# A Mamba block and a mixture of experts on one core: a new table of steps for the work beside the scan

## The chip, the core and the metric

The kernel runs on one core of a Trainium2 chip, in one launch. The metric is the device time of the launch in microseconds, lower is better. Everything is float32.

## The reference, cut to what matters

```python
# x: (8, 1024, 256); _layernorm without g, b is plain, with eps 1e-5
x = x + attn_block(_layernorm(x))
x = x + ffn_block(_layernorm(x))

# attn_block(x): Di = 512, 16 states, rank 64, 4 taps
h = _layernorm(x, ln_g, ln_b)
x_in, z = split(h @ W_in)
x_c = silu(causal_depthwise_conv(x_in, conv_w, conv_b))
dt, Bm, Cm = split(x_c @ W_xproj, [64, 80])
delta = softplus(dt @ W_dt + b_dt)
s = exp(delta * A) * s + delta * Bm * x_c          # along the sequence
y = sum(s * Cm, over the 16 states) + x_c * D_param
return x + (y * silu(z)) @ W_out

# ffn_block(x): 8 experts, the best 2 of each row, softmax over the two
logits = x @ Wg + bg
y = x + sum of w_e * (relu(x @ W1[e] + b1[e]) @ W2[e] + b2[e])
return gamma * (y - mean) * rsqrt(var + 1e-5) + beta
```

## The kernel before, in words

**Chunks, groups, steps.** The 8192 rows are cut into 16 chunks of 512. Even chunks begin a sequence and odd ones go on with it, so the states' last column is kept (`carry`) in an even chunk and read in the odd one. A chunk has 4 groups of 128 channels, a group has 16 states, and one state of one group is a step: 64 steps a chunk, 1024 in all. Each engine's program is one loop over the steps (`for at in range(STEPS)`, GpSimd over half-steps of two), and every other piece of work is put between the steps by a constant. Engines run each their own program; they meet at semaphores only, so a step number is a place in an engine's order and not a time.

**A step.** ScalarE makes the decay, `exp(delta * a)` (`exp_a`, L1156). GpSimd makes the drive, two states at a time (`times_b`, L852); for the states 4, 5, 10 and 11 TensorE does so with diagonal matrices (`drive`, L1462, at the group's steps 4 and 10; a chunk has its drives at 4, 10, 20, 26, 36, 42, 52, 58). VectorE scans (`scan`, L664). It then multiplies five pairs of states of a group by C (`weigh`, L676), and GpSimd the other three pairs (L869, behind a copy of the carry, L863). TensorE turns each pair and adds it up in `ps_y` (`turn_d`, L1435, `turn_p`, L1445; `TURN_D` and `TURN_P` say at which step), after `begin_y` (L1426) has put the skip term there. VectorE gates the sum at the next group's step 3 (`gate`, L686). State 0 reuses the bank of state 15, so ScalarE can't start a group before VectorE has scanned the last state of the one before.

**Work beside the steps.** `STEADY` lists the projections and turns of a chunk as (kind, g, chunk relative to the current one, TensorE's first step, in how many parts, how many steps after it ScalarE takes the result out). Kinds: h (the normalised rows turned, L1318), x and z (L1324, L1328), conv (four taps as matmuls, L1335), dbc and bturn (dt, B, C; B turned for the diagonals), dt (L1346), turnu (delta*u turned for the drives, L1381), back (the gated rows turned back, L1390), out (L1400, L1404), turnx, logit (L1353, L1357, L1361) and rank (the router's). The list is sorted by first step plus parts, and its results take turns in the two banks of `ps_p`: a use waits until the one two places before it has been taken out (`project`, `emptied`). In the last step before 64 a copy may fall into the next chunk.

**The other constants.** `NORM`, `STATS`, `INV_STD`: the first layer norm of the chunk two ahead. `ADD_DT`: the last softplus step on VectorE. `SILU_U`, `SILU_Z`: SiLU with two loads of ScalarE's table each. `XL_AT`: the residual. `STATS_X1`, `INV_STD_X1`, `FACTOR_X1`, `XN`: squares, reciprocal deviation, the product for the offset (`factors_x1`, L818, GpSimd, counted in half-steps) and the normalisation (`normalise_x1`, L1001) of the last chunk's rows before the router. `ROUTE`: VectorE's fourteen small router instructions (`route_step`, L592 to L619), the steps of each; from one to the next it waits on its own semaphore. `EXP_W`, `IDS_0`, `IDS_1`, `SCATTER`: the two weights, the rows' numbers, and the stores of the rows by expert. `DIAGONALS`: the diagonal matrices of B (`diagonals`, L1109), four parts. `HALO_AT`: the three columns that the convolution needs of the chunk before. They are written out as numbers; nothing in the kernel reckons costs or due times. `RESIDUAL` is read nowhere.

The loops that place the work on ScalarE look like this:

```python
for kind, g, q, at, parts, lag in table:
    if at >= 0 and kind in (...):
        empty_at.setdefault(at + lag, []).append((kind, g, q))
# in the loop over the steps: empties first, then the norms, last
for k in keep_at.get(at, ()):
    keep(k)
exp_a(c, s // N, s % N)
```

Of the kernel before, what the change touches and what calls it, by code (L numbers as in the profile page):

```python
# [111 lines left out]
def mamba_block(nc, x_t, x1_t, b_dram, ln_g, ln_b, W_in, conv_w, conv_b, W_xproj, W_dt, b_dt, A_log, D_param,  # L112
# [25 lines left out]
    with ExitStack() as ctx:  # L138
        def sb(name, shape, dt=F32):
            return ctx.enter_context(nc.sbuf_tensor(name, shape, dt))  # L140

        def sem(name):
# [30 lines left out]
        dbc = sb("dbc", [K_DT, CH])  # L173
# [108 lines left out]
        OUT_EARLY = NC * SG - 5  # L282
        SPIN_FIRST = {"dbc": 8, "bturn": 3, "turnu": 12}
        SPIN_LAST = {"out": 4, "turnx": 14, "logit": 4, "rank": 4}
        STEADY = [("h", 0, 1, 0, 1, 3), ("h", 1, 1, 1, 1, 5), ("back", 3, -1, 6, 1, 3), ("x", 0, 1, 7, 2, 3),
                  ("dt", 2, 0, 8, 1, 2), ("out", 0, -1, 11, 2, 3), ("turnu", 1, 0, 12, 1, 4), ("x", 1, 1, 14, 1, 6),
                  ("out", 1, -1, 16, 2, 6), ("x", 2, 1, 21, 1, 3), ("conv", 0, 1, 22, 1, 2), ("x", 3, 1, 23, 2, 2),
                  ("conv", 1, 1, 23, 4, 6), ("dt", 3, 0, 27, 1, 3), ("conv", 2, 1, 27, 3, 5),
                  ("turnu", 2, 0, 34, 1, 2), ("conv", 3, 1, 32, 4, 7), ("turnx", 0, -1, 37, 1, 4),
                  ("turnx", 1, -1, 37, 1, 4), ("logit", 0, -1, 40, 1, 4), ("dbc", 0, 1, 41, 1, 3),  # L290
                  ("bturn", 0, 1, 42, 1, 4), ("back", 1, 0, 42, 1, 4), ("rank", 0, -1, 44, 1, 0),
# [3 lines left out]
        HALO_AT = 0  # L295
        XL_AT = 11
        SILU_U = 41
        SILU_Z = 73
        NORM = (54, 58)
        ADD_DT = ((49, 0), (51, 1), (74, 2), (95, 3))  # L300
        RESIDUAL = ((10, 0), (4, 1))
        STATS = (47, 48)
        INV_STD = (51, 54, 55)
        FACTOR = 28
        STATS_X1 = (26, 27)
        INV_STD_X1 = (28, 28)
        FACTOR_X1 = 17
        XN = (34, 38)
        ROUTE = (38, 39, 40, 40, 40, 41, 41, 41, 41, 41, 45, 45, 45, 45)
        EXP_W = (44, 46, 46)  # L310
        IDS_0 = 46
        IDS_1 = 58
        SCATTER = ((25, 0, 0), (25, 0, 1), (27, 0, 2), (28, 0, 3), (32, 1, 0), (33, 1, 1), (35, 1, 2), (38, 1, 3))
        DIAGONALS = (54, 57, 61, 63)
        DRIVE = (4, 4, 10, 10)
        KEEP_EARLY = (4, 9)
        GATE = 3
        TURN_D = {9: 0, 11: 1, 14: 2, 15: 3, 19: 4}
        TURN_P = {9: 0, 15: 1, 20: 2}
        SKIP_Y = 7  # L320
        WEIGH_P = {5: 0, 8: 1, 10: 2}
# [3 lines left out]
        def due(at, offset, d, span=SG):  # L325

            c, rest = divmod(at - offset, span)
            return c + d if rest == 0 and 0 <= c + d < NC else None

        uses = sorted([(*u, 0) for u in START] + [(*u, NC - 1) for u in END] + [(*u, None) for u in STEADY],  # L330
                      key=lambda u: u[3] + u[4])
# [228 lines left out]
        def _(dve):  # L560
# [179 lines left out]
            for at in range(STEPS):  # L740
# [19 lines left out]
                for j, offset in enumerate(STATS):  # L760
                    q = due(at, offset, 2)
                    if q is not None:
                        (stats_a, stats_b)[j](q)
                for j, offset in enumerate(ROUTE):
                    q = due(at, offset, -1)
# [33 lines left out]
        def _(pool):  # L799
# [9 lines left out]
            def factors(q):  # L809

                pool.wait_ge(rs_done, 3 * q + 2)
                pool.tensor_tensor(nb[:, q % 3], rr[:, q % 3], nm[:, 0, :].unsqueeze(1).broadcast_to([P, 2, NT]),
                                   ALU.mult).then_inc(prm, 1)

            def factors_x1(q):

                pool.wait_ge(rsr_done, 2 * q + 2)
                pool.tensor_tensor(x_ln[:, 1, :], x_ln[:, 0, :], nm[:, 1, :], ALU.mult).then_inc(prm1, 1)  # L818
# [56 lines left out]
            for at in range(STEPS // 2):  # L875
# [20 lines left out]
                if q is not None and q > 1:  # L896
                    factors(q)
                q = due(at, FACTOR_X1, -1, G * HB)
                if q is not None:
                    factors_x1(q)  # L900
                for offset, k, i in SCATTER:
                    q = due(at, offset, -1, G * HB)
# [4 lines left out]
        def _(act):  # L907
            def set_halo(q):

                if q > 0:  # L910
                    act.wait_ge(proj_full, full("conv", 3, q - 1))
                if q == 1:
                    act.wait_ge(conv_step, TAPS * (G - 1))
                if q % 2 == 0:
                    act.memzero(xin[:, :, 0:HALO]).then_inc(halo, 1)
                else:
                    act.copy(xin[:, :, 0:HALO], xin[:, :, CH:CH + HALO]).then_inc(halo, 1)
# [314 lines left out]
            for at in range(STEPS):  # L1232
                c, s = divmod(at, SG)
                if s == HALO_AT and c + 1 < NC:
                    set_halo(c + 1)
# [19 lines left out]
                if q is not None:  # L1255
                    silu_gate(q)
                    act.preload_act_table_set("natural_log_exp_and_others")
                for j, offset in enumerate(INV_STD):
                    q = due(at, offset, 2)
                    if q is not None:  # L1260
                        inv_std(q, j)
                for j, offset in enumerate(STATS_X1):
                    q = due(at, offset, -1)
                    if q is not None:
                        stats_x1(q, j)
                for j, offset in enumerate(INV_STD_X1):
                    q = due(at, offset, -1)
                    if q is not None:
                        inv_std_x1(q, j)
                if s in NORM and c + 2 < NC:  # L1270
                    normalise(c + 2, range(2) if s == NORM[0] else range(2, NT))
                if s in XN and 0 < c <= NC and at != NC * SG + XN[1]:
                    normalise_x1(c - 1, range(2) if s == XN[0] else range(2, NT))
                for j, offset in enumerate(EXP_W):
                    q = due(at, offset, -1)
                    if q is not None:
                        weight_exp(q, j)
                for j, offset in enumerate(START_DIAGONALS):
                    if at == offset:
                        diagonals(0, 2 + j)  # L1280
                for j, offset in enumerate(DIAGONALS):
                    q = due(at, offset, 1)
                    if q:
                        diagonals(q, j)
                for k, offset in enumerate((IDS_0, IDS_1 if at < NC * SG else IDS_0)):
                    q = due(at, offset, -1)
# [13 lines left out]
        def _(pe):  # L1300
# [165 lines left out]
            def turns(t, n):  # L1466

                if 0 < t <= LAST + 1:
                    if n + N in TURN_D:
                        turn_d(t - 1, TURN_D[n + N])  # L1470
                    if n + N in TURN_P:
                        turn_p(t - 1, TURN_P[n + N])
                if t <= LAST:
# [3 lines left out]
                    if n == SKIP_Y:  # L1477
                        begin_y(t)
                    if n in TURN_D:
                        turn_d(t, TURN_D[n])  # L1480
                    if n in TURN_P:
# [445 lines left out]
```

## Time and profile before

| what | us |
|---|---|
| three runs | 2424.89, 2426.41, 2429.95 |
| median | 2426.41 |
| profiled execution | 2419.56 |
| its span | 2417.9 |
| VectorE, busy in the span | 2039.6 |
| TensorE (matmuls), busy | 2179.0 |
| GpSimd, busy | 1829.7 |
| ScalarE, busy | 1511.6 |

The span goes from the first to the last instruction of the profiled execution, and its time has some 2 us more around it. The busy shares are an average over two parts that are unlike: the scan up to 1802 us and, behind it, the experts, which TensorE fills. In the rows below PE is TensorE, PEld its weight loads, DVE VectorE, ACT ScalarE, POOL GpSimd. A bracket behind a row of a timeline is the time for which the engine was idle before it, and who ended that. The chunks are numbered from 0; chunk 6 starts at 706.10 us, chunk 7 at 815.33 us and chunk 8 at 926.12 us (VectorE's scan of step 0).

### The profile page before, as it was taken

How to read it: one execution, taken by the hardware profiler on the slowest of the kernel's cores; microseconds unless marked ns; L12 is line 12 of the kernel's file. 1: busy time of each engine (PE TensorE's matmuls, PEld its weight loads, DVE VectorE, ACT ScalarE, POOL GpSimd, SP SyncE). 2: the span in 40 equal slices, each digit the busy share in tenths (PEclk: the TensorE clock that was granted, in tenths of full speed). 3: DMA queues.
4: the chain of work that ended last, by engine and by line, in shares of the span. 5: the costliest groups of instructions: out<-in, count | busy, mean ns of one | idle time of the engine just before them, and what ended most of it. 6: DMA issues, size and time to landing. Idle time of an engine off the chain costs nothing. (4 is left out here: it accounts for less than half of the span.)

```text
span 2417.9 us, 47511 instructions
## 1 busy us (share of the span) xinstructions
PE 2179.0 (90%) x13721; PEld 1761.9 (73%) x13722; DVE 2039.6 (84%) x3049; ACT 1511.6 (63%) x3296; POOL 1829.7 (76%) x1093
## 2 busy tenths in 40 slices
PE   8889899998989899998989898999787999999980
PEld 5667677776767777766777776667676999999970
DVE  5999999999999999999999999999984555555558
ACT  6687877878787877878787878778741111111106
POOL 3888989889898989898898989898972444444447
PEclk9999999999999999999999999999988999999995
DMA  5041423314041413223140413132238999999978
GB/s 173 9 134 50 136 69 108 114 63 159 27 158 38 139 61 125 93 83 137 47 158 22 156 50 136 64 112 100 69 111 222 229 233 226 232 227 228 230 165 278
DMA packets 186792, 312.51 MB, mean 129 GB/s; under 512 B 18851, under 2 KB 118083, under 8 KB 186500
## 3 DMA queue, kind: packets, MB, share of 16 engines
q1 hardware_dynamic: 140932, 258.53, 33.8%
q0 software_dynamic: 25584, 34.62, 7.5%
q10 hardware_dynamic: 20112, 17.32, 2.2%
q8 instruction: 85, 1.39, 0.2%
q14 instruction: 79, 0.65, 0.1%
HBM read 247.09 MB, written 63.32 MB: 128 GB/s over the span
## 5 line engine op out<-in xcount | busy, mean ns | idle before, releaser
L852 POOL TENSOR_TENSOR dbu<-drive_u,b_rows 128x1024 f32<-128x1024 f32 x384 | 905.1, 2365 | 82.9 <-DVE ss L664 32.2
L1156 ACT ACTIVATE ps_a<-delta,a_neg 128x512 f32<-128x512 f32 x768 | 518.1, 687 | 136.9 <-DVE ss L664 120.4
L869 POOL TENSOR_TENSOR wp<-ss,rows_c 128x1024 f32<-128x1024 f32 x192 | 454.0, 2364 | 35.8 <-DVE ss L664 35.2
L1764 POOL DMA_INDIRECT acc_scratch<-ow,idx x135 | 212.1, 1571 | 306.5 <-issue 140.0
L676 DVE TENSOR_TENSOR wd<-ps_a,rows_c 128x1024 f32<-128x1024 f32 x320 | 385.6, 1205 | 0.0
L1435 PEld LDWEIGHTS ps_y<-ident,wd 128*128 128x128 f32 x2560 | 299.8, 143 | 100.0 <-issue 71.0
L1435 PE MATMUL ps_y<-ident,wd 128*128 128x128 f32 x2560 | 337.2, 277 | 13.5 <-DVE wd L676 13.2
L1802 ACT COPY e_meta<-xt 128x2 f32<-128x2 f32 x135 | 26.1, 193 | 437.4 <-PE e_ps_x L1875 250.5
L1462 PEld LDWEIGHTS ps_a<-dg,duT 128*128 128x128 f32 x2048 | 251.8, 198 | 56.8 <-issue 55.5
L1462 PE MATMUL ps_a<-dg,duT 128*128 128x128 f32 x2048 | 261.4, 283 | 29.8 <-ACT carry L1163 27.3
L1686 DVE TENSOR_SCALAR e_hT<-e_ps_h,b_turned 128x128 f32<-128x128 f32 x540 | 152.1, 345 | 142.0 <-PE e_ps_h L1884 124.5
L1884 PE MATMUL e_ps_h<-xT,b_rows 128*128 128x128 f32 x2160 | 263.3, 275 | 0.3 <-ACT xT L1804 0.3
L1893 PE MATMUL e_ps_o<-rows_c,e_hT 128*128 x1080 | 255.3, 379 | 0.0
L664 DVE TENSOR_TENSOR_SCAN ss<-ps_a,carry,dbu 128x512 f32<-128x512 f32 x192 | 243.9, 1270 | 11.5 <-ACT ps_a L1156 11.5
L1884 PEld LDWEIGHTS e_ps_h<-xT,b_rows 128*128 128x128 f32 x2160 | 251.9, 192 | 0.6 <-ACT xT L1804 0.6
L664 DVE TENSOR_TENSOR_SCAN ss<-ps_a,dbu 128x512 f32<-128x512 f32 x192 | 232.1, 1209 | 22.6 <-ACT ps_a L1156 20.6
L664 DVE TENSOR_TENSOR_SCAN ps_a<-ps_a,carry,dbu 128x512 f32<-128x512 f32 x192 | 238.8, 1282 | 0.7 <-issue 0.6
L664 DVE TENSOR_TENSOR_SCAN ps_a<-ps_a,dbu 128x512 f32<-128x512 f32 x192 | 227.6, 1220 | 9.1 <-ACT ps_a L1156 7.2
L1335 PE MATMUL ps_p<-xin,taps 128*128 128x512 f32 x488 | 231.9, 593 | 0.8 <-ACT xin L1053 0.8
L1445 PE MATMUL ps_y<-ident,wp 128*128 128x128 f32 x1536 | 206.4, 279 | 15.7 <-POOL wp L869 15.0
L1893 PEld LDWEIGHTS e_ps_o<-rows_c,e_hT 128*128 128x128 f32 x1080 | 194.9, 190 | 21.0
L1445 PEld LDWEIGHTS ps_y<-ident,wp 128*128 128x128 f32 x1536 | 178.1, 143 | 30.9 <-POOL wp L869 22.9
(200 smaller groups left out, 3650.9 us busy)
## 6 DMA issues: line engine op xcount, KB each, us to landing
b_rows<-in_L_ffn_W_dram SPq DMA_DIRECT2D x135, 512.0 KB
rows_c<-b_scratch SPq DMA_DIRECT2D x128, 512.0 KB, 5.1
b_rows<-b_scratch SPq DMA_DIRECT2D x96, 512.0 KB, 4.1
xt<-xs_scratch SPq DMA_DIRECT2D x135, 129.0 KB
xb<-in_L_attn_x_dram SPq DMA_DIRECT2D x16, 512.0 KB, 4.0
hx<-in_L_attn_x_dram SPq DMA_DIRECT2D x16, 512.0 KB, 6.4
x_scratch<-hx SPq DMA_DIRECT2D x16, 512.0 KB, 2.9
acc_scratch<-stage SPq DMA_DIRECT2D x16, 512.0 KB, 2.9
```

What stands on the lines that cost most here:

```text
L664: dve.tensor_tensor_scan(dst, decay, drive, init, ALU.mult, ALU.add).then_inc(scan_done, 1)
L676: dve.tensor_tensor(wd[:, s % NWD], states(k, 2), cc[:, n:n + 2, :], ALU.mult).then_inc(wd_done, 1)
L852: pool.tensor_tensor(dbu[:, k % NBU], du[:, g % 2, :].unsqueeze(1).broadcast_to([P, 2, CH]), bb[:, row:row + 2, :], ALU.mult).then_inc(dbu ...
L869: pool.tensor_tensor(wp[:, s % 2], ss[:, s % 2], cc[:, rows, :], ALU.mult).then_inc(wp_done, 1)
L1156: act.activation(dst, dl[:, g, :], ACT.Exp, scale=a_neg[:, g, n:n + 1]).then_inc(exp_done, 1)
L1335: ins = pe.matmul(dst, taps[:, g, k, :], xin[:, g, k:k + CH], start=(k == 0), stop=(k == TAPS - 1))
L1435: ins = pe.matmul(ps_y[:, i, :], wd[:, s % NWD, h, i * P:(i + 1) * P], ident[:], start=False, stop=False, is_transpose=True, skip_group_ch ...
L1445: ins = pe.matmul(ps_y[:, i, :], wp[:, s % 2, h, i * P:(i + 1) * P], ident[:], start=False, stop=(j == 2 and h == 1 and i == NT - 1), is_t ...
L1462: ins = pe.matmul(ps_a[:, bank(k), i * P:(i + 1) * P], duT[:, i, :], dg[:, p, h, i, :], start=True, stop=True)
L1764: pool.indirect_dma_start(out=acc_dram, out_offset=bass.IndirectOffsetOnAxis(ap=idx[:, old, :], axis=0), in_=ow[:, old, :], in_offset=None ...
L1884: ins = pe.matmul(ps_h[:, 1 - par, j, :], w1[:, (slot + 3) % RING, k, j * P:(j + 1) * P], xT[:, 1 - par, k, :], start=(k == 0), stop=(k == ...
L1893: ins = pe.matmul(ps_o[:, par, 0:D], hT[:, par, k, :], w2[:, bass.ds((e * KF + k) * D, D)], start=(k == 0), stop=(k == KF - 1))
```

## The change

It alters constants in the table of steps and nothing else: which step of a chunk each piece of work has in its engine's order, in how many parts TensorE does it, and how many steps later ScalarE takes it out. No instruction's operands change, and none is added or taken away, but for where a projection is cut into parts.

```diff
--- before.py
+++ after.py
@@ -282,40 +282,40 @@
         OUT_EARLY = NC * SG - 5
         SPIN_FIRST = {"dbc": 8, "bturn": 3, "turnu": 12}
         SPIN_LAST = {"out": 4, "turnx": 14, "logit": 4, "rank": 4}
-        STEADY = [("h", 0, 1, 0, 1, 3), ("h", 1, 1, 1, 1, 5), ("back", 3, -1, 6, 1, 3), ("x", 0, 1, 7, 2, 3),
-                  ("dt", 2, 0, 8, 1, 2), ("out", 0, -1, 11, 2, 3), ("turnu", 1, 0, 12, 1, 4), ("x", 1, 1, 14, 1, 6),
-                  ("out", 1, -1, 16, 2, 6), ("x", 2, 1, 21, 1, 3), ("conv", 0, 1, 22, 1, 2), ("x", 3, 1, 23, 2, 2),
-                  ("conv", 1, 1, 23, 4, 6), ("dt", 3, 0, 27, 1, 3), ("conv", 2, 1, 27, 3, 5),
-                  ("turnu", 2, 0, 34, 1, 2), ("conv", 3, 1, 32, 4, 7), ("turnx", 0, -1, 37, 1, 4),
-                  ("turnx", 1, -1, 37, 1, 4), ("logit", 0, -1, 40, 1, 4), ("dbc", 0, 1, 41, 1, 3),
-                  ("bturn", 0, 1, 42, 1, 4), ("back", 1, 0, 42, 1, 4), ("rank", 0, -1, 44, 1, 0),
-                  ("back", 0, 0, 45, 1, 2), ("turnu", 3, 0, 46, 1, 2), ("dt", 0, 1, 48, 1, 0), ("dt", 1, 1, 49, 1, 3),
-                  ("z", 0, 1, 54, 1, 1), ("z", 1, 1, 57, 1, 2), ("z", 2, 1, 58, 2, 6), ("turnu", 0, 1, 60, 1, 2),
-                  ("back", 2, 0, 62, 1, 4), ("z", 3, 1, 61, 2, 5)]
-        HALO_AT = 0
+        STEADY = [("h", 0, 1, 0, 1, 3), ("h", 1, 1, 0, 1, 5), ("back", 3, -1, 6, 1, 3), ("x", 0, 1, 7, 2, 3),
+                  ("dt", 2, 0, 8, 1, 2), ("out", 0, -1, 11, 1, 2), ("turnu", 1, 0, 12, 1, 4), ("x", 1, 1, 14, 1, 6),
+                  ("out", 1, -1, 15, 2, 6), ("x", 2, 1, 20, 1, 3), ("conv", 0, 1, 22, 1, 3), ("x", 3, 1, 23, 2, 2),
+                  ("conv", 1, 1, 23, 4, 6), ("dt", 3, 0, 26, 1, 3), ("conv", 2, 1, 27, 3, 5),
+                  ("turnu", 2, 0, 34, 1, 3), ("conv", 3, 1, 31, 4, 7), ("turnx", 0, -1, 37, 1, 4),
+                  ("turnx", 1, -1, 37, 1, 4), ("logit", 0, -1, 39, 1, 5), ("dbc", 0, 1, 41, 1, 4),
+                  ("back", 1, 0, 42, 1, 4), ("rank", 0, -1, 42, 1, 0), ("back", 0, 0, 46, 1, 2),
+                  ("turnu", 3, 0, 46, 1, 2), ("bturn", 0, 1, 47, 1, 3), ("dt", 0, 1, 49, 1, 0),
+                  ("dt", 1, 1, 49, 1, 3), ("z", 0, 1, 54, 1, 1), ("z", 1, 1, 54, 2, 3), ("turnu", 0, 1, 58, 1, 2),
+                  ("z", 2, 1, 58, 2, 6), ("back", 2, 0, 60, 1, 3), ("z", 3, 1, 60, 2, 5)]
+        HALO_AT = 5
         XL_AT = 11
         SILU_U = 41
         SILU_Z = 73
-        NORM = (54, 58)
+        NORM = (55, 58)
         ADD_DT = ((49, 0), (51, 1), (74, 2), (95, 3))
-        RESIDUAL = ((10, 0), (4, 1))
+        RESIDUAL = ((10, 0), (0, 1))
         STATS = (47, 48)
-        INV_STD = (51, 54, 55)
+        INV_STD = (53, 54, 54)
         FACTOR = 28
-        STATS_X1 = (26, 27)
-        INV_STD_X1 = (28, 28)
-        FACTOR_X1 = 17
-        XN = (34, 38)
-        ROUTE = (38, 39, 40, 40, 40, 41, 41, 41, 41, 41, 45, 45, 45, 45)
-        EXP_W = (44, 46, 46)
-        IDS_0 = 46
-        IDS_1 = 58
-        SCATTER = ((25, 0, 0), (25, 0, 1), (27, 0, 2), (28, 0, 3), (32, 1, 0), (33, 1, 1), (35, 1, 2), (38, 1, 3))
-        DIAGONALS = (54, 57, 61, 63)
+        STATS_X1 = (25, 26)
+        INV_STD_X1 = (26, 27)
+        FACTOR_X1 = 18
+        XN = (35, 37)
+        ROUTE = (38, 40, 40, 40, 40, 41, 41, 41, 41, 41, 45, 45, 45, 45)
+        EXP_W = (44, 46, 47)
+        IDS_0 = 47
+        IDS_1 = 59
+        SCATTER = ((25, 0, 0), (25, 0, 1), (26, 0, 2), (27, 0, 3), (32, 1, 0), (33, 1, 1), (35, 1, 2), (38, 1, 3))
+        DIAGONALS = (54, 57, 61, 64)
         DRIVE = (4, 4, 10, 10)
         KEEP_EARLY = (4, 9)
         GATE = 3
-        TURN_D = {9: 0, 11: 1, 14: 2, 15: 3, 19: 4}
+        TURN_D = {9: 0, 11: 1, 12: 2, 18: 3, 20: 4}
         TURN_P = {9: 0, 15: 1, 20: 2}
         SKIP_Y = 7
         WEIGH_P = {5: 0, 8: 1, 10: 2}
```

## Rows read from the trace of the kernel before

**Rows 1.** one stretch: length, busy us of PE, PEld, DVE, ACT, POOL, PEclk, DMA

```profile
40.00:1802.00 1762.00, 1617.15 (x9871) 1246.39 (x9872) 1670.84 (x1791) 1373.31 (x2830) 1555.40 (x881) 0.98 0.28 95
```

**Rows 2.** waits of VectorE, 40 to 1802: us in total, times, longest

```profile
DVE ss L664 <- ACT ps_a L1156: 32.1, 21, 2.1
DVE delta L636 <- ACT delta L1127: 26.1, 16, 3.0
DVE ps_a L664 <- PE ps_a L1462: 13.5, 17, 1.4
...
DVE mx L592 <- PE ps_p L1361: 3.4, 8, 0.8
DVE ps_a L664 <- POOL dbu L852: 1.8, 1, 1.8
```

**Rows 3.** timeline, VectorE, chunk 6: start, us, what [idle before]

```profile
745.38 1.23 DVE L664 TENSOR_TENSOR_SCAN ps_a<-ps_a,dbu 128x512 f32<-128x512 f32 x1 [0.59 <-ACT ps_a L1156]
748.75 1.22 DVE L664 TENSOR_TENSOR_SCAN ss<-ps_a,dbu 128x512 f32<-128x512 f32 x1 [2.14 <-ACT ps_a L1156]
...
751.83 2.34 DVE L664 TENSOR_TENSOR_SCAN ps_a<-dbu,ps_a 128x512 f32<-128x512 f32 x2 [0.74 <-PE ps_a L1462]
...
772.84 0.19 DVE L592 TENSOR_REDUCE mx<-ps_p 128x4 f32<-128x32 f32 x1 [0.38 <-PE ps_p L1361]
...
774.08 0.17 DVE L594 TENSOR_TENSOR ps_p<-ps_p,mx 128x32 f32<-128x32 f32 x1
774.16 1.22 DVE L664 TENSOR_TENSOR_SCAN ps_a<-ps_a,dbu 128x512 f32<-128x512 f32 x1
```

**Rows 4.** timeline, TensorE, chunk 6, drives of steps 10 and 26

```profile
718.97 2.02 PE L1462 MATMUL ps_a<-dg,duT 128*128 128x128 f32 x16 [0.58 <-ACT carry L1163]
...
750.74 1.95 PE L1462 MATMUL ps_a<-dg,duT 128*128 128x128 f32 x16
```

**Rows 5.** timeline, GpSimd, chunk 6 and chunk 7

```profile
757.22 0.19 POOL L818 TENSOR_TENSOR x_ln<-x_ln,nm 128x4 f32<-128x4 f32 x1
...
759.96 2.37 POOL L869 TENSOR_TENSOR wp<-ss,rows_c 128x1024 f32<-128x1024 f32 x1
...
869.48 2.37 POOL L869 TENSOR_TENSOR wp<-ss,rows_c 128x1024 f32<-128x1024 f32 x1 [2.93 <-DVE ss L664]
```

**Rows 6.** timeline, ScalarE, chunk 6 and chunk 7

```profile
761.36 1.08 ACT L1001 ACTIVATE stage<-hx,x_ln 128x256 f32<-128x256 f32 x2
762.35 1.29 ACT L1156 ACTIVATE ps_a<-delta,a_neg 128x512 f32<-128x512 f32 x2
...
769.23 1.07 ACT L1076 COPY xb<-ps_p 128x512 f32<-128x512 f32 x2 [0.17 <-PE ps_p L1353]
...
870.74 1.09 ACT L1001 ACTIVATE stage<-hx,x_ln 128x256 f32<-128x256 f32 x2
...
878.51 1.07 ACT L1076 COPY xb<-ps_p 128x512 f32<-128x512 f32 x2 [0.15 <-PE ps_p L1353]
```

**Rows 7.** timeline, TensorE, chunk 6, first matmul of the logits

```profile
770.45 0.40 PE L1357 MATMUL ps_p<-bgb,ones 1*128 1x32 f32 x2
```

**Rows 8.** timeline, VectorE, behind the scan

```profile
1819.55 0.20 DVE L594 TENSOR_TENSOR ps_p<-ps_p,mx 128x32 f32<-128x32 f32 x1
1819.78 0.22 DVE L596 TENSOR_TENSOR_SCAN cn<-first,ps_p 128x32 f32<-128x32 f32 x1
```

**Rows 9.** timeline, TensorE, starts of chunks 6 and 8

```profile
707.06 1.14 PE L1318 MATMUL ps_p<-ident,hx 128*128 128x128 f32 x8 [1.90 <-ACT zt L1098]
...
927.08 1.45 PE L1318 MATMUL ps_p<-ident,hx 128*128 128x128 f32 x8 [1.91 <-ACT zt L1098]
```

**Rows 10.** timeline, VectorE, chunk 8, steps 4 and 9

```profile
931.72 0.69 DVE L686 TENSOR_TENSOR zt<-ps_y,zt 128x512 f32<-128x512 f32 x1
932.56 2.34 DVE L664 TENSOR_TENSOR_SCAN ps_a<-dbu,ps_a 128x512 f32<-128x512 f32 x2
...
939.80 1.22 DVE L664 TENSOR_TENSOR_SCAN ss<-ps_a,dbu 128x512 f32<-128x512 f32 x1 [0.43 <-ACT ps_a L1156]
```

## The prediction

> **What bounds the kernel now.** I read the stretches first: the scan runs from 40 to 1802 us, VectorE is busy for 1670.8 of those 1762 us and TensorE for 1617.2 [rows 1]. None of the changed constants acts on the experts behind it, which fill the rest of the span, so they are costed at nothing. The scan is 16 chunks of 64 steps, some 110 us each, and what can move is the 91 us in which VectorE is idle (1762 less 1670.8) and whatever the new order adds. The waits of VectorE say who ends them [rows 2]: ScalarE's exponentials (32.1 us), the softplus of dt 2 (26.1), TensorE's drive products (13.5), the router's logits (3.4). GpSimd ended one wait of a drive, 1.8 us: it is ahead, and its moved scatters cost nothing as long as that lead stands.
>
> The timeline of VectorE shows the places in one chunk (chunk 6, even; all even chunks look alike, and the odd ones nearly so) [rows 3]: at step 25 it waits 2.14 us for ScalarE, at step 26 another 0.74 us for TensorE, at step 38 0.38 us for the logits. TensorE's timeline tells what stands behind the first two [rows 4]. It waits once, 0.58 us for a carry copy behind SiLU, starts the drive at 718.97, and from there works without a break to the drive of step 26 at 750.74, on which the scan at 751.83 starts. The wait at step 25 lies inside this chain. Were it gone, VectorE would reach step 26 earlier and wait there instead. So up to step 26 a chunk is as long as TensorE's work, and only work taken out of that chain, or a wait put into it, counts.
>
> **The change part by part.** (1) *Steps 0 to 26.* x 2, out 0 and out 1 come a step earlier, turn 3 moves behind out 1 (15 to 18), turn 4 from 19 to 20, turn 2 from 14 to 12. Between the drive of step 10 and that of step 26 TensorE issues the same instructions as before in another order; no work leaves the chain. conv 0 is evacuated one ScalarE step later, so the exponential of step 24 no longer waits for it: its wait was inside the chain, worth nothing. STATS_X1 a step earlier puts four squares and a logarithm ahead of the exponential of step 26. That exponential now comes about level with the drive instead of well ahead of it. I take nothing, between nothing and the 0.74 us that VectorE waits there now, and nearer to nothing because the four squares and the logarithm together are hardly longer than the lead.
>
> (2) *The router's row factor.* FACTOR_X1 goes from GpSimd's half-step 17 to 18. At 17 it stood behind a product and ran at 757.22. At 18 it is issued behind the weighing of the third staged pair, which waits for the scan of step 31 and runs at 759.96 for 2.37 us, in the odd chunk at 869.48 [rows 5]. So it is done at 762.53 (759.96 + 2.37 + 0.20), in the odd chunk at 872.05. XN (34 to 35) waits for it. ScalarE began that normalisation at 761.36 and 870.74 [rows 6]: it is now 1.17 and 1.31 us late. Against this, one exponential (a pair takes 1.29 us, so 0.6 from start to start) now runs ahead of it, and the waits of 0.17 and 0.15 us before the copies of the turned rows are used up [rows 6]. That leaves 0.40 and 0.56 us. The logits' first matmul began at 770.45, 0.15 us after the copies' end at 770.30 (769.23 + 1.07), of which I count 0.1 as slack [rows 6, 7]: 0.30 and 0.46 us. I take 0.30 for both, since in the odd chunk ScalarE has more small waits to use up. VectorE waits for the logits already (0.38 us in rows 3), and in odd chunks they land with nothing to spare, so this is wholly exposed: 14 chunks x 0.30 = 4.2 us. Queued behind VectorE's maximum are the scans of 39 to 41. Bounds: 0 if ScalarE finds the time elsewhere, 14 x 0.46 = 6.4 us.
>
> (3) *ROUTE 39 to 40.* The compare with the maximum stood between two scans, independent of both: 774.08 to 774.16, 0.08 us [rows 3]. Now the router's next instruction, which reads its result and waits for its semaphore, stands directly behind it. That pair occurs at the end of the scan, 1819.55 to 1819.78: 0.23 us [rows 8]. So 0.15 us more on VectorE in each of 15 chunks: 2.25 us. Bounds: 0 and 15 x 0.23 = 3.5 us.
> The Trainium skill, page "VectorE: DVE Perf Modes", section "The DRAIN you can't avoid", says otherwise: a chain of vector operations with a semaphore after each took as long as one without, since the next has to wait for the pipe anyway. By it this part is 0 and the sum below 2.5 us; rows 3 and 8 speak against it, with two spacings for the same instruction.
>
> (4) *The end of a chunk and the start of the next.* z 1 goes from 57 to 54 in two parts, turn u 0 from 60 to 58, back 2 from 62 to 60 and its copy from ScalarE's step 2 to 63, h 1 from 1 to 0, the last diagonals from 63 to 64, halo to 5. At the start of an even chunk TensorE waited 1.90 us for the copy of back 2 (at 707.06). In chunks 4, 8 and 12 its granted clock then fell to the lower level: in chunk 8 the same eight turns took 1.45 us instead of 1.14 [rows 9], the drive came late, and VectorE lost 0.15 us at step 4 (the gate ends at 932.41, the scan starts at 932.56) and 0.43 at step 9 [rows 10]. With that copy made before the chunk ends h 0 doesn't wait; h 1 does, for z 3's copy, but 0.5 us less. I take the 0.58 us as gained in these three chunks: -1.7 us. Bounds: 0 and 7 x 0.58 = -4.1 us. The softplus wait of step 10 stays: SiLU and the residual hold it, and both start from the exponentials behind the weighing of step 3, which neither moves.
>
> (5) *Slots.* Projections alternate between two banks, so a new order gives new predecessors. dt 1 now waits for the copy of bturn (ScalarE's step 50), z 1 for the softplus sum of dt 1 on VectorE (step 51), z 3 for the copy of z 2 (step 0 of the next chunk), behind which stand turn 3, the turns of h and the drive of step 4. By the order of these steps TensorE waits a step or two in each place, where it waited as long elsewhere; none is on the path as long as the clock stays up. NORM, INV_STD, bturn, back 0, EXP_W and IDS move by one step or more on a ScalarE that is then a little ahead. rank two steps earlier, logit one: TensorE's order around them is unchanged where it binds. dbc's copy a step later delays SyncE's store of B and C and the loads queued behind it by a microsecond or two; the rows are wanted a third of a chunk later. All this I cost at 0. If the cover goes, it is rival A.
>
> Sum: 4.2 + 2.25 - 1.7 = +4.7 us. The profiled execution took 2419.56 us (its span 2417.9), 6.9 us below the median of the three runs, 2426.41. The terms are stalls that repeat in each chunk, so I add them to the median: **2431.1 us**. A measurement of this kernel can tell about 0.2%, 4.9 us, from no change; the forecast lies just inside that.
>
> **The rivals.** *A, slower.* The longer waits in (5) lower TensorE's clock just before the drive of step 4 in most chunks, not in three. The price is that of chunk 8, 0.58 us [rows 10], and a further 0.3 (1.45 less 1.14, rows 9) because the eight matmuls of turn 3 now stand in front of that drive as well: 0.9 x 14 = 12.6 us without the gain in (4), so 2426.4 + 6.4 + 12.6 = 2445 us if in all chunks, 2439 if in half. It decides from the point where the drive of step 4 is over 0.6 us later than now. For it: row 927.08. Against it: in four of seven even chunks the clock stayed up after a wait as long.
> The Trainium skill, page "TensorE: Matmul & The Clock Gate", section "HAM oscillation", says that gaps in matmul work bring the clock down to half each time; here it fell after one of the two waits in rows 9.
> *B, faster.* ScalarE, not TensorE, sets steps 24 to 26: the modelled ends of matmuls are late, the drive of step 26 is in fact ready, and conv 0 out of the way gives back what it cost. Even chunks wait 0.59 us at step 24 [rows 3]: 7 x 0.6 = 4.2 us, and the 0.74 us at step 26 shrink by half, 14 x 0.37 = 5.2. With the sum, 2431.1 - 9.4 = 2421.7 us. For it: the 32.1 us put down to ScalarE [rows 2]. Against it: TensorE's unbroken row [rows 4].
> *C, the order doesn't matter.* The positions have slack everywhere except in places that don't change, and the late logits are caught up by the waits of steps 41 and 42: 2426 us. The waits' regularity speaks against it.
> *D*, part (3) costs nothing: 2428.9 us.
>
> **How the numbers follow.** Forecast 0.33 (about half of it on either side of +0.2%), A 0.22, B 0.20, C 0.17, D 0.08. Faster is B and the low edge: 0.21. Within 0.2%: C, D and half of the forecast: 0.41. Slower: A and the other half, 0.38. The range reaches down to B, 2420, and up to A in half of the chunks, 2439.
>
> **What would show it.** In the changed kernel's trace: the drives of step 26 end in the same distance from step 3 (TensorE's row unbroken), VectorE's waits for logits rise from 3.4 to some 8 us in odd chunks too, GpSimd's small product of the row factor stands behind the weighing, the compare is 0.23 us ahead of the next router instruction, and the turns of h wait less than 1.9 us. Step 24 waits for nothing. It is wrong if chunks get shorter before step 26, or if the wait of step 4 grows in every chunk (A).

## The result, and the profile after

The changed kernel takes 2434.01 us (median of 7 runs, 2431.55 to 2436.24), the kernel before, run beside it, 2422.9 us (7 runs with the three shown above, 2420.47 to 2429.95). The ratio is 1.0037, 95% interval [1.0027, 1.0048]: slower by 9 us of 2423. (The medians of the two sets of seven are 11 us apart; where the two differ I go by the ratio and its interval.) The forecast was +4.7 us.

The profiled execution took 2431.55 us, its span 2429.8 against 2417.9. The first row has the busy times of the whole span. The second is the stretch of the scan, which now ends at 1812 instead of 1802 (columns as in [rows 1]).

```profile
PE 2190.3 (90%) x13721; PEld 1767.1 (73%) x13722; DVE 2040.4 (84%) x3049; ACT 1506.2 (62%) x3296; POOL 1827.0 (75%) x1093
```

```profile
40.00:1812.00 1772.00, 1626.91 (x9875) 1249.99 (x9876) 1671.89 (x1792) 1368.54 (x2831) 1553.70 (x880) 0.97 0.28 94
```

VectorE is busy for 1671.9 us where it was busy for 1670.8: of the 10 us more, 9 are waits. TensorE is busy for 10 us more with the same matmuls, and the mean granted clock is 0.97 instead of 0.98: those matmuls were slower. VectorE's waits up to 1812 us say where it shows (to be read against [rows 2]):

```profile
DVE ss L664 <- ACT ps_a L1156: 38.6, 19, 3.3
DVE delta L636 <- ACT delta L1127: 28.1, 18, 3.4
DVE ps_a L664 <- PE ps_a L1462: 18.4, 21, 1.5
...
DVE mx L592 <- PE ps_p L1361: 3.9, 8, 0.5
```

The first row has grown by 6.5 us, for the most part because the wait of step 25 took over those of step 24, as forecast in part (1). The third is new time: four waits more, 4.9 us more, the longest 1.5 us. To place it, I took the distance from the start of each of the 1024 scans of a step to the next in both traces and subtracted. All together are 10.2 us longer; by place in the chunk, summed over the 16 chunks:

| from the scan of step to the next | us | in which chunks |
|---|---|---|
| 41 to 42 (waits for the drive) | +7.4 | +1.36 in 3, +1.54 in 8, 10, 12, 14; 1 had it already |
| 39 to 41 (the compare) | +2.0 | 0.14 in each of 15 |
| 38 to 39 (the logits) | +1.6 | +0.09 to +0.18 in 1 to 14, -0.27 in 15 |
| 35 to 36 | +1.3 | +0.16 in even ones |
| 23 to 26 | +1.0 | +1.8 in 0, else -0.2 to +0.02 |
| 56 to 57 | +1.1 | 0, 2, 4 |
| 10 to 11 | -2.1 | -1.8 in 0 |
| 3 to 4 and 8 to 9 | -1.9 | -0.57 in 4, 8, 12 |

The rest adds up to -0.2 us, and behind the scan come 1.7 us more that no run looked into. The -1.8 us of chunk 0 stands in e1 below too, whose one change comes later than that, so it isn't the new order's. One place, which the prediction doesn't name, holds most of the difference between these two executions. This is TensorE's timeline there, in chunk 8 of the changed kernel, and VectorE's scan of step 42:

```profile
993.01 1.06 PE L1426 MATMUL ps_y<-skipd,xc 128*128 128x128 f32 x8
994.12 0.37 PE L1357 MATMUL ps_p<-bgb,ones 1*128 1x32 f32 x2
994.42 1.95 PE L1361 MATMUL ps_p<-wg,xb 128*128 128x8 f32 x16
996.23 1.07 PE L1435 MATMUL ps_y<-ident,wd 128*128 128x128 f32 x8
997.14 1.80 PE L1445 MATMUL ps_y<-ident,wp 128*128 128x128 f32 x8
998.74 4.56 PE L1341 MATMUL ps_p<-xc,wxp 128*96 128x512 f32 x8
1003.13 1.95 PE L1462 MATMUL ps_a<-dg,duT 128*128 128x128 f32 x16
```

```profile
1004.22 2.34 DVE L664 TENSOR_TENSOR_SCAN ps_a<-dbu,ps_a 128x512 f32<-128x512 f32 x2 [1.46 <-PE ps_a L1462]
```

In chunk 6, where nothing is lost, the turns of wp and the projection dbc take their usual times:

```profile
776.86 1.04 PE L1445 MATMUL ps_y<-ident,wp 128*128 128x128 f32 x8
777.74 3.60 PE L1341 MATMUL ps_p<-xc,wxp 128*96 128x512 f32 x8
```

So 0.76 us (1.80 less 1.04) and 0.96 us (4.56 less 3.60) are lost in a row, ahead of the drive that VectorE needs next. Two stretches of chunk 8, before the slow matmuls and over them (the last columns are the granted clock, the DMA share and GB/s):

```profile
993.80:997.20 3.40, 3.35 (x30) 3.15 (x29) 2.93 (x4) 3.37 (x3) 2.71 (x2) 1.00 0.00 0
997.25:1000.66 3.41, 3.41 (x12) 2.27 (x11) 3.31 (x7) 3.26 (x5) 2.35 (x1) 0.50 0.00 0
```

TensorE's clock is at its upper level of 2.4 GHz, then at the lower one, 1.2 GHz. TensorE did not wait before that, being busy for 3.35 of 3.40 us; but what it did were the logits, sixteen records with 8 moving columns each. The Trainium skill, page "TensorE: Matmul & The Clock Gate", section "HAM oscillation", ties the fall to idle gaps between matmuls; this row has next to no gap, so the trace doesn't agree. The kernel before has the same event once, in chunk 1 (dbc 4.77 us, a wait of 1.4 us, the "longest" of the third line of [rows 2]); the changed kernel has it in six chunks.

### The profile page after: what moved, and what is told of

Read it like the earlier page. It is cut to its first block and busy times, and to the rows that moved or that the text cites. A ratio compares the mean times of both kernels' runs of the same rounds, so it can differ in the third digit from the quotient of the medians.

```text
span 2429.8 us, 47511 instructions
## 1 busy us (share of the span) xinstructions
PE 2190.3 (90%) x13721; PEld 1767.1 (73%) x13722; DVE 2040.4 (84%) x3049; ACT 1506.2 (62%) x3296; POOL 1827.0 (75%) x1093
## 5 line engine op out<-in xcount | busy, mean ns | idle before, releaser
L1435 PE MATMUL ps_y<-ident,wd 128*128 128x128 f32 x2560 | 331.9, 278 | 8.6 <-DVE wd L676 8.0
L1462 PEld LDWEIGHTS ps_a<-dg,duT 128*128 128x128 f32 x2048 | 244.6, 194 | 35.8 <-issue 34.2
L1462 PE MATMUL ps_a<-dg,duT 128*128 128x128 f32 x2048 | 255.1, 278 | 15.1 <-ACT carry L1163 10.9
L1445 PE MATMUL ps_y<-ident,wp 128*128 128x128 f32 x1536 | 209.8, 282 | 13.2 <-POOL wp L869 13.2
L1445 PEld LDWEIGHTS ps_y<-ident,wp 128*128 128x128 f32 x1536 | 183.2, 146 | 43.6 <-issue 23.7
```

The costliest lines, as they stand in the source:

```text
L1435: ins = pe.matmul(ps_y[:, i, :], wd[:, s % NWD, h, i * P:(i + 1) * P], ident[:], start=False, stop=False, is_transpose=True, skip_group_ch ...
L1445: ins = pe.matmul(ps_y[:, i, :], wp[:, s % 2, h, i * P:(i + 1) * P], ident[:], start=False, stop=(j == 2 and h == 1 and i == NT - 1), is_t ...
L1462: ins = pe.matmul(ps_a[:, bank(k), i * P:(i + 1) * P], duT[:, i, :], dg[:, p, h, i, :], start=True, stop=True)
```

## The experiments

Each kernel was profiled in one execution, and chunks are counted in that one; how the count varies between executions of a kernel was not seen. Two theories. **Order**: TensorE's new order around steps 39 to 42 makes the clock fall. **Alignment**: the thin logits can bring the clock down in any of these kernels, and whether they do in a given chunk depends on when they come, so that any small shift changes the number of chunks hit. The first four kernels share 22 runs of the kernel before (median 2423.61 us, 2419.53 to 2427.11).

**e1, the compare alone.** Kernel before with

```diff
-        ROUTE = (38, 39, 40, 40, 40, 41, 41, 41, 41, 41, 45, 45, 45, 45)
+        ROUTE = (38, 40, 40, 40, 40, 41, 41, 41, 41, 41, 45, 45, 45, 45)
```

> The kernel before with the router's second instruction moved from step 39 to 40, nothing else. In the changed kernel VectorE needs about 0.14 us more at steps 40 and 41 of each chunk, and in six chunks TensorE's clock is low over step 41 and costs 1.4 to 1.5 us at step 42. Theory Alignment (the thin matmuls of the logits can lower the clock in any of these kernels; whether they do depends on when the stretch comes, which every small shift alters): 15 x 0.15 = +2.2 us from the instruction, and the places where the clock is low move; with low clock at step 41 in several chunks up to +7 us more. Theory Order (the new order of TensorE's work makes the stretch prone to it): +2.2 us and low clock at step 41 in chunk 1 only, as before.

2425.47 us, ratio 1.0007 [0.9997, 1.0017]. The scans of steps 39 and 40 are 0.08 us closer, those of 40 and 41 0.22 us further apart, in each of 15 chunks: +2.0 us. Part (3) stands. Two chunks (2 and 10) have the wait of 1.5 us at step 42, where the kernel before had one.

**e2, the row factor alone.** Kernel before with

```diff
-        FACTOR_X1 = 17
-        XN = (34, 38)
+        FACTOR_X1 = 18
+        XN = (35, 37)
```

> The kernel before with FACTOR_X1 at 18 and XN at 35 and 37, nothing else. My part (2): the logits come 0.3 us later in 14 chunks, +4.2 us. The changed kernel's trace shows only some 0.2 us at steps 36 to 39, so by its rows +2 to +3 us. Theory Alignment: low clock at step 41 in some chunks is possible here too, each +1.5 us; theory Order: none but chunk 1.

2432.85 us, ratio 1.0042 [1.0029, 1.0055]: as large as the whole loss, with TensorE's order untouched. (The profiled execution, 2437.66 us, was the slowest of its seven, that of the kernel before one of its fastest, so the two profiles lie further apart than the ratio.) Its chunk 6, GpSimd's factor, ScalarE's normalisation and VectorE's maximum:

```profile
763.31 2.38 POOL L869 TENSOR_TENSOR wp<-ss,rows_c 128x1024 f32<-128x1024 f32 x1
765.65 0.20 POOL L818 TENSOR_TENSOR x_ln<-x_ln,nm 128x4 f32<-128x4 f32 x1
...
765.89 1.09 ACT L1001 ACTIVATE stage<-hx,x_ln 128x256 f32<-128x256 f32 x2 [0.49 <-POOL x_ln L818]
...
776.47 0.19 DVE L592 TENSOR_REDUCE mx<-ps_p 128x4 f32<-128x32 f32 x1 [0.65 <-PE ps_p L1361]
```

The factor stands behind the weighing, as forecast, and the logits are waited for 0.65 us instead of 0.38 [rows 3]: 0.27 us more in even chunks, 0.19 in odd ones, 3.2 us in all. The other 11.7 us are at step 42, in chunks 2, 4, 6, 8, 10, 12 and 14 (1.67 us each; chunk 1 has it as before):

```profile
996.25 0.37 PE L1357 MATMUL ps_p<-bgb,ones 1*128 1x32 f32 x2 [0.24 <-ACT xb L1076]
996.55 1.95 PE L1361 MATMUL ps_p<-wg,xb 128*128 128x8 f32 x16
998.36 1.26 PE L1435 MATMUL ps_y<-ident,wd 128*128 128x128 f32 x8
999.41 1.92 PE L1445 MATMUL ps_y<-ident,wp 128*128 128x128 f32 x8
1001.12 4.29 PE L1341 MATMUL ps_p<-xc,wxp 128*96 128x512 f32 x8
```

```profile
999.10:1002.51 3.41, 3.41 (x14) 2.59 (x12) 3.34 (x7) 3.38 (x6) 2.35 (x1) 0.50 0.00 0
```

The theory Order falls: in this execution the old order is hit in eight chunks, behind a shift of 0.2 to 0.3 us.

**e3, all but those two.** Changed kernel with ROUTE, FACTOR_X1 and XN as before.

> The changed kernel with ROUTE, FACTOR_X1 and XN as before; the whole order of TensorE's work stays new. Theory Order: low clock at step 41 stays in five or six chunks, so only the two small parts come back, -2 to -4 us against the changed kernel, still 6 us or more above the kernel before. Theory Alignment: a chunk is 0.15 to 0.45 us shorter, the stretch comes at other times, and the number of chunks with low clock there is free to change, to none or to more; without any the time is within 2 us of the kernel before.

2427.68 us, ratio 1.0017 [1.0007, 1.0026], with the wait in five chunks (1, 8, 10, 12, 14), which both theories allow. Nothing is paid between steps 39 and 41; the logits come as before in even chunks and 0.16 us later in odd ones, which some other move does.

**e4, the end of a chunk alone.** Kernel before with h 1, z 1, turn u 0, back 2, z 3, HALO_AT, NORM, INV_STD, IDS_1 and the last of DIAGONALS as after.

> The kernel before with the changes at a chunk's end alone (h 1, z 1, z 3, turn u 0, back 2, halo, diagonals, NORM, INV_STD, IDS_1). My part (4): the waits of steps 4 and 9 in chunks 4, 8 and 12 go, -1.7 us. Theory Alignment: the places of low clock move from the drive of step 52 and the turns of h to others, and may fall on step 41. Theory Order, if the new chunk end is what brings the low clock to step 41: it shows there in several chunks, +5 us or more; if it is not, none but chunk 1.

2450.71 us, ratio 1.0108 [1.0085, 1.0131]. Step 42 costs 9.6 us more (seven chunks, again with the old order around it), and another 21 us stand between steps 0 and 3. TensorE in chunk 8, waiting for ScalarE to empty z's bank (L1057), the stretch behind that wait (columns as above), and VectorE:

```profile
936.51 3.78 PE L1328 MATMUL ps_p<-win,turned_h 128*128 128x512 f32 x4 [3.58 <-ACT zt L1057]
```

```profile
936.50:940.30 3.80, 3.79 (x5) 1.61 (x6) 3.80 (x5) 1.83 (x5) 3.60 (x3) 0.50 0.94 340
```

```profile
945.68 1.22 DVE L664 TENSOR_TENSOR_SCAN ss<-ps_a,dbu 128x512 f32<-128x512 f32 x1 [1.79 <-ACT ps_a L1156]
```

The waits for slots of part (5) are real when the end of the chunk is changed alone. Behind this one the clock is low as well, and the four records of z take 3.78 us, where the changed kernel's took 1.98 behind a wait of 2.86 us (at 704.82); how the 21 us divide between wait and clock was not taken apart. In the whole change something else covers them. Which move does was not tried.

The next four kernels share 17 runs of the kernel before (2424.58 us, 2420.21 to 2430.05). They act on the consequence (dbc out of the way of the drive) and on the cause (dense work at the logits).

**g1, dbc behind the drive.** Changed kernel with

```diff
-                  ("dbc", 0, 1, 41, 1, 4),
+                  ("dbc", 0, 1, 42, 1, 3),
```

> The changed kernel with dbc issued one step later (42, its copy still in ScalarE's step 45), so that it stands behind the drive of step 42 and not ahead of it. Theory 'thin logits' (TensorE's clock falls in the stretch of the 8-column logits matmuls of step 39, and dbc, 3.60 us at the upper level and 4.56 at the lower, and the drive behind it are on VectorE's path): VectorE's waits of 1.54 us at step 42 go; five of them are 7.7 us, so about 2434.0 - 7.7 = 2426 us. Rival 'placement elsewhere' (the 10 us come from the order as a whole and step 42 only shows them): the wait moves to another step and the time stays at 2433 to 2436 us.

2433.17 us, ratio 1.004 [1.0028, 1.0052]. All waits of step 42 are gone (-9.0 us), and the time isn't: the stretch from step 44 to 50 takes it back, most of it in chunks 8, 10, 12 and 14. Chunk 8 again, TensorE, the clock before and after 1006.95, and VectorE:

```profile
1004.22 1.04 PE L1375 MATMUL ps_p<-sel,ones 128*128 128x32 f32 x8
...
1005.33 1.04 PE L1375 MATMUL ps_p<-sel,ones 128*128 128x32 f32 x8
1006.23 2.98 PE L1435 MATMUL ps_y<-ident,wd 128*128 128x128 f32 x16
...
1014.68 1.12 PE L1346 MATMUL ps_p<-dbc,wdt 97*128 97x512 f32 x2 [1.68 <-ACT bT L1088]
```

```profile
1003.53:1006.93 3.40, 3.18 (x29) 3.18 (x30) 3.40 (x5) 3.12 (x10) 3.15 (x2) 1.00 0.49 120
1006.95:1010.37 3.42, 3.42 (x19) 3.42 (x17) 3.39 (x8) 0.27 (x1) 2.24 (x4) 0.50 0.77 218
```

```profile
1014.51 1.23 DVE L664 TENSOR_TENSOR_SCAN ps_a<-ps_a,dbu 128x512 f32<-128x512 f32 x1 [0.90 <-ACT ps_a L1156]
1016.32 0.69 DVE L636 SCALAR_TENSOR_TENSOR delta<-ps_p,delta 128x512 f32<-128x512 f32 x1 [0.58 <-ACT delta L1127]
```

The clock now falls behind the next thin matmuls, those of rank (32 columns). The expectation of 2426 us failed; the wait moved.

**g2, the same on the kernel before**; and **g3, the same on e2.**

> The kernel before with dbc at 42 instead of 41. Both theories agree nearly: the kernel before lost only 1.4 us at step 42, in chunk 1. 'Thin logits': 0 to -1.5 us, 2421 to 2424 us, and none of the waits at step 42 over 1 us. 'Placement elsewhere': the same or slower, since dbc's copy is a step later.

> The kernel before with FACTOR_X1 at 18 and XN a step later, which gave 2432.9 us with eight waits of 1.6 us at step 42, now with dbc at 42. 'Thin logits': the eight waits go whether or not the clock falls there, 2432.9 - 12.5 = 2420 us, with the part of the later normalisation (about +1.5) within it: 2420 to 2424 us. 'Placement elsewhere': it stays at 2430 us or more.

g2: 2437.67 us, ratio 1.0049 [1.0034, 1.0063]. g3: 2443.61 us, 1.0076 [1.0052, 1.01]. Both expectations failed, though the waits at step 42 are gone in both (-1.6 and -13.2 us). I had left out what is queued behind dbc in the old order: bturn reads dbc's copy, and rank stands behind bturn. TensorE and VectorE of g2 in chunk 8:

```profile
1011.23 0.40 PE L1385 MATMUL ps_p<-ident,dbc 32*128 32x32 f32 x4 [0.76 <-ACT dbc L1070]
```

```profile
1015.55 0.22 DVE L611 TENSOR_TENSOR pick<-sel,ps_p 128x64 f32<-128x64 f32 x1 [2.13 <-PE ps_p L1375]
```

From step 45 to 46 g2 loses 14.8 us, g3 19.0. That is not the queue alone. In the even chunks from 2 to 14 whose clock stayed up behind the logits the loss is 1.42 to 1.51 us (four chunks of the two kernels), and 0 in such odd ones; where the clock fell there it is 1.88 to 2.23 us in even chunks (ten) and 1.56 to 1.60 in odd ones (four). So the moved projection costs some 1.5 us in even chunks by its queue, and the low clock, which is still there in five and nine chunks, is paid for at step 46 instead of 42: 0.4 to 0.8 us in even chunks and 1.6 in odd ones.

**g4, dense work ahead of the logits.** e2 with

```diff
+                    for _ in range(2):
+                        pe.matmul(dst[:, 128:512], ident[:], win[:, 0, 0:384], start=True, stop=True,
+                                  skip_group_check=True)
                     pe.matmul(dst[:, 0:NT * E], ones[0:1, :], bgb[:]...
```

> The kernel before with FACTOR_X1 at 18 and XN a step later, and two extra matmuls of 384 columns (their result lands in unused columns of the logits' bank and is read by nobody) ahead of each chunk's logits matmuls. 'Thin logits': with dense work in front the granted clock stays at its upper level over steps 39 to 41, so that the waits of 1.6 us at step 42 go, in exchange for about 1.3 us more of TensorE's work in each chunk, part of which shows as a longer wait for the logits (step 38 or 39) or for the drive of step 42: the low-clock stretches at step 39 vanish, the time is 2420 to 2440 us. Rival 'the clock falls whatever is issued there': as many low-clock stretches at steps 39 to 41 as without, and 2432.9 + 10 to 20 us.

2451.08 us, ratio 1.0101 [1.0077, 1.0124]. The logits come 1.48 us later in each chunk, and the clock still falls in six of chunks 1 to 14 (2, 3, 5, 8, 9, 14). Chunk 9:

```profile
1116.70 1.53 PE L1358 MATMUL ps_p<-win,ident 128*128 128x384 f32 x4 [0.16 <-ACT xb L1076]
1118.16 0.40 PE L1360 MATMUL ps_p<-bgb,ones 1*128 1x32 f32 x2
1118.49 1.95 PE L1364 MATMUL ps_p<-wg,xb 128*128 128x8 f32 x16
...
1122.57 4.80 PE L1341 MATMUL ps_p<-xc,wxp 128*96 128x512 f32 x8
```

```profile
1118.15:1121.55 3.40, 3.40 (x31) 3.35 (x31) 1.78 (x3) 3.37 (x4) 1.11 (x1) 1.00 0.00 0
1121.57:1124.97 3.40, 3.40 (x10) 1.85 (x8) 3.33 (x8) 1.56 (x3) 2.35 (x1) 0.50 0.02 5
```

"No low clock" failed, and the time came where the rival had put it (10 to 20 us above 2432.9). Either the fall has nothing to do with the logits, or dense work in front doesn't help and the logits themselves have to be dense. There is also no wait of TensorE in these 3.40 us, which speaks against its small wait for the logits (0.16 to 0.24 us) as the cause.

That can be tried at hardly any cost, because the 8-column records of the logits and the 128-column records of a drive both take 1.95 us for sixteen. In i1 to i3 and j1 each logits matmul reads its 8 columns sixteen times; only the first 8 results are used:

```diff
-                            ins = pe.matmul(dst[:, i * E:(i + 1) * E], rT[:, k, i * P:(i + 1) * P], wg[:, k, :],
+                            ins = pe.matmul(dst.rearrange("p (r c) -> p r c", c=NT * E)[:, :, i * E:(i + 1) * E],
+                                            rT[:, k, i * P:(i + 1) * P], wg[:, k, :].unsqueeze(1).broadcast_to([P, 16, E]),
```

**i1, the changed kernel so; i2, e2 so; i3, e3 so** (27 runs of the kernel before beside them, 2424.43 us, 2419.41 to 2429.74).

> The changed kernel with its logits matmuls made 128 columns wide instead of 8 (the 8 columns of router weights read sixteen times; the fifteen extra results land in columns of the bank that nobody reads). The 128-column drive matmuls take 1.95 us for sixteen records, just as the 8-column logits do, so the work is hardly longer. Theory 'thin logits': no stretch of the lower clock between steps 39 and 42 any more, no wait of 1.5 us at step 42, 2434.0 - 9.0 = 2425 us; if the fall moves to a later router stretch, as with dbc at 42, there is a second wait behind it and less is gained. Rival 'the lower clock comes there whatever TensorE does' (the widened dense matmuls ahead of the logits did not stop it): as many stretches as before, 2434 us or a little more.

> The kernel before with FACTOR_X1 at 18 and XN a step later, which had the lower clock behind the logits in 8 of 15 chunks and gave 2432.9 us, with the logits matmuls 128 columns wide. Theory 'thin logits': none of the eight, 2432.9 - 13.2 = 2420 us. Rival: eight of them, 2433 us.

> The changed kernel with ROUTE, FACTOR_X1 and XN of the kernel before (2427.7 us, five waits at step 42 of about 1.6 us) and the logits matmuls 128 columns wide. Theory 'thin logits': the five go, 2427.7 - 8 = 2420 us, faster than both kernels. Rival: 2428 us.

i1: 2422.75 us, 0.9993 [0.9984, 1.0002]. i2: 2422.05 us, 0.9988 [0.9979, 0.9997]. i3: 2418.9 us, 0.998 [0.9971, 0.9989]. All three came out near the forecasts of the thin logits (2425, 2420, 2420) and 9 to 11 us below the rivals'. i1, chunk 8:

```profile
991.66 2.05 PE L1361 MATMUL ps_p<-wg,xb 128*128 128x128 f32 x16
993.55 1.03 PE L1436 MATMUL ps_y<-ident,wd 128*128 128x128 f32 x8
994.43 1.04 PE L1446 MATMUL ps_y<-ident,wp 128*128 128x128 f32 x8
995.30 3.60 PE L1341 MATMUL ps_p<-xc,wxp 128*96 128x512 f32 x8
```

```profile
991.20:998.00 6.80, 6.73 (x42) 5.03 (x42) 6.11 (x10) 6.50 (x8) 4.88 (x3) 1.00 0.00 0
998.00:1003.00 5.00, 5.00 (x41) 4.30 (x39) 4.93 (x10) 3.18 (x9) 4.68 (x3) 1.00 0.14 19
```

The clock stays up, dbc takes 3.60 us, and VectorE's waits for the drives, up to 1802 us, are 10.3 us where the changed kernel has 18.4:

```profile
DVE ps_a L664 <- PE ps_a L1463: 10.3, 16, 0.7
```

Scan by scan, against the kernel without wide logits: i1 -8.9 us ahead of step 42 and +0.10 us per chunk ahead of step 39, i2 -13.25 and +0.10, i3 -8.2 and +0.10. Between steps 38 and 42 of chunks 1 to 14 no stretch of the lower clock is left in the profiled executions, where the same three without it had 6, 8 and 5. The wide logits are also a shift, of 0.10 us, and shifts move these stretches. But each of the ten profiled kernels with thin logits has one to nine of them whatever was shifted, and the four with wide logits (j1 below is the fourth) have none, so the shift is an unlikely cause.

**j1, the kernel before so** (16 runs beside it, 2424.83 us, 2420.59 to 2431.7).

> The kernel before, with its logits matmuls 128 columns wide and nothing else. The 27 runs of it beside the last three kernels lie between 2419.4 and 2429.7 us, the 11 of each widened kernel within 2.9 to 4.5 us. Theory 'thin logits': that spread is the number of chunks in which the lower clock meets the drive of step 42, so that its median of 2424.4 contains two or three such waits, though its profile shows one; widened, its runs are within some 4 us and the median is at the low end of its range plus the 1.5 us that the wide matmuls cost, less one wait: 2419 to 2421 us. Then i3's gain over the kernel before is the widening and little else. Rival 'the gain of i3 came from the new order': the median stays at 2422 to 2424 us and 3 to 5 us above i3.

2418.62 us (2416.14 to 2421.78), ratio 0.9975 [0.9964, 0.9986], no wait of that kind. It beats the kernel before by 6 us, and with i3 it is the fastest of all. So what i3 gained came from the width, not from the new order.

j1 and i1 also tell what the change costs with the event taken out of both kernels: 2422.75 less 2418.62, 4.1 us (4.4 by the two ratios, each of which is known to 2 or 3 us). i3 is only 0.3 us above j1, so this is the compare and the row factor. Of the 9 us about half is the shifts themselves and about half more low clock at step 42; the two profiles alone, 7.4 of 10.2 us, put the event's part too high.

## Why the prediction was right or wrong

The sign and the range were right, the size came out at about half. The absolute 2431.1 us flatters the forecast: it starts from a median of three runs, 2426.41, that seven put at 2422.9. As differences, +4.7 us were forecast and +9.0 measured (+6.5 to +11.6 by the ratio's interval).

- **Part (1), steps 0 to 26 at nothing: right.** In even chunks the wait of step 24 is 0.69 us shorter, that of step 25 0.79 longer, that of step 26 0.08 shorter: +0.02.
- **Part (2), the row factor, 0.30 us per chunk: right alone, not in company.** e2 shows 0.27 and 0.19 us, 3.2 us against 4.2. On top of the other moves (changed kernel against e3) it is 0.10 and 0.01, some 0.8 us: other moves have made the logits or the scan ahead of them 0.16 us late already, and the two together give e2's 0.27 and 0.19 within 0.02. The step that failed is "wholly exposed". Those other moves brought 0.16 us of their own (35 to 36 in even chunks, 38 to 39 in odd ones), which I had at 0.
- **Part (3), the compare, 0.15 us: right**, 0.14 in each of 15 chunks in e1 and in the changed kernel. The Trainium skill, page "VectorE: DVE Perf Modes", section "The DRAIN you can't avoid", says that a chain of copies with a semaphore behind each took no longer than one without. By that rule this part would have been 0; for this pair the runs speak against it.
- **Part (4), -1.7 us: the size right, the reason open.** Chunks 4, 8 and 12 gain 0.57 us each at steps 4 and 9. But e2, which leaves the end of the chunk alone, gains the same in the same chunks, so a shift is enough. For the prediction's reason: in the six profiled kernels with the new end of a chunk the clock never falls at steps 0 to 3 of chunks 1 to 14, and in seven of the eight with the old end it does, in one to three chunks. It falls at steps 60 to 63 instead, in six chunks of the changed kernel. That much of rival A came true, but not its price: step 4 loses nothing.
- **Part (5), slots at nothing:** held in the whole change (steps 1 to 3 lose nothing from chunk 1 on), not in e4. There the wait of 3.58 us is some two steps long, as expected, but the clock is low behind it and VectorE waits too.
- **The missing term: 7.4 us at step 42 in the profiled execution, some 5 by the times of i1 and j1.** No step of the sum asks where the clock may fall behind the logits. Rival A had the mechanism, "the longer waits lower TensorE's clock just before the drive", but at the drive of step 4, behind idle time, and at 0.9 us. It happened at step 42, behind busy but thin matmuls, at 1.36 to 1.67 us, because 3.60 us of dbc stand in the slow stretch ahead of the drive. [Rows 2] held the hint: a longest wait of 1.4 us for a drive, which I did not look up.

That the change with the event taken out costs 4.1 to 4.4 us, close to the sum of 4.7, is in part luck: the row factor gives 0.8 us instead of 4.2, moves that stood at 0 give 0.16 us in nearly each chunk, some 2.4 us, and the -1.7 us may be any shift's.

B fell: between steps 23 and 26 odd chunks gained at most 0.2 us, even ones nothing. C fell: neither the later logits nor the compare was wholly caught up. D fell with e1.

The scatter of the kernel before fits the same cause, as far as these runs go. Beside e1 to j1 its runs spread over 7.6 to 11.1 us, those of the four widened kernels over 2.9 to 5.6 us, and its profiled execution, one of its fastest, had one wait of 1.4 us. The mean granted clock, known for 82 of its runs, goes with their times: the 33 with 0.966 or more have a median of 2421.8 us, the 14 with 0.961 or less one of 2427.1. So its slow executions have more low clock; that they have it at step 42 was not seen, since only one of them was profiled. Open as well: which move covers the slots of e4, and whether rank, made wide in the same way, would be worth anything. The clock still falls behind rank or near it in i1 to i3, where steps 43 to 57 of a chunk with it are longer than those of one without by 0.3 us at most; that was not tried.

## What to carry to other kernels

Look at the granted clock over the stretch ahead of each wait for TensorE, not only behind idle time: here it fell behind a row of busy matmuls with few moving columns, and the price depends on what stands between it and the next result that someone needs. Where a matmul of 8 columns takes as long as one of 128, widen it with columns nobody reads. And when several small shifts each "cost" several us in a pattern over the chunks, suspect one event that they move, and remove the event from both kernels before judging the shifts.

## What was not expected of the hardware

- TensorE's clock fell to 1.2 GHz while TensorE was busy for 3.35 of the 3.40 us before it (g4: 3.40 of 3.40), behind 8-column logits. Such falls stand in 55 of 140 chunks (chunks 1 to 14 of the ten profiled kernels with thin logits), and in 0 of 56 with 128 columns. In 33 of the 55 TensorE was busy without a break for 3.4 us before, in the others for 3.18 us at least.
- Width is nearly free: 2.05 us for sixteen records of 128 columns against 1.95 of 8.
- Two 384-column matmuls (four records, 1.53 us) right ahead of the thin ones did not keep the clock up.
- With the same instructions in each chunk, a shift of 0.2 to 0.3 us took the number of chunks hit from one to eight, 11.7 us of waits, in one profiled execution of each kernel; by the times of all runs the two kernels are 10 us apart.
